# A decoder layer on one NeuronCore: the row of maxima of the cross-attention written by one VectorE step over seven rows of contraction

## What is computed

```python
q = (query @ Wq + bq).reshape(B, Nq, H, D).transpose(0, 2, 1, 3)
k = (key_value @ Wk + bk).reshape(B, Nkv, H, D).transpose(0, 2, 1, 3)
v = (key_value @ Wv + bv).reshape(B, Nkv, H, D).transpose(0, 2, 1, 3)
attn = jnp.einsum('bhqd,bhkd->bhqk', q, k) * scale
attn = jnp.clip(attn, -CLAMP, CLAMP)
attn = jax.nn.softmax(attn, axis=-1)
x = jnp.einsum('bhqk,bhkd->bqhd', attn, v).reshape(B, Nq, Cq)
return x @ Wo + bo
```

## Time and profile before

| | us |
|---|---|
| median of 3 runs | 972.74 |
| lowest, highest | 971.3, 974.29 |
| the profiled execution, its own time | 974.64 |
| its span in the trace | 972.5 |
| TensorE busy | 924.9 (95%) |
| VectorE busy | 699.5 (72%) |
| ScalarE busy | 645.9 (66%) |
| GpSimd busy | 351.0 (36%) |

### The profile page before, as it was taken

How to read it: one execution, slowest core, us unless ns; L and a number is a source line. 1 busy time by engine, 2 the same in 40 slices (tenths; PEclk the granted TensorE clock), 3 DMA queues, 4 the chain that set the end, 5 groups by cost and what they waited for, 6 DMA issues and landing times.

```text
span 972.5 us, 28783 instructions
## 1 busy us (share of the span) xinstructions
PE 924.9 (95%) x10471; PEld 741.4 (76%) x10471; DVE 699.5 (72%) x1490; ACT 645.9 (66%) x1081; POOL 351.0 (36%) x332
## 2 busy tenths in 40 slices
PE   6777999999999999999999999999999999999995
PEld 4655777777777777777777777777777778999894
DVE  6673777767676677676767767767788857777996
ACT  4654777777777777777777777777776545445554
POOL 6452362222333333222233333332222413112992
PEclk8897999999999999999999999999999999999998
DMA  5538566666655555666666555566665201002321
GB/s 141 121 79 191 120 133 140 143 136 137 137 128 119 119 119 126 141 137 138 136 137 134 119 119 119 120 137 143 137 138 111 69 1 44 23 23 86 128 114 41
DMA packets 43626, 111.44 MB, mean 115 GB/s; under 512 B 15491, under 2 KB 26053, under 8 KB 43461
## 3 DMA queue, kind: packets, MB, share of 16 engines
q1 hardware_dynamic: 43572, 110.77, 50.3%
HBM read 32.23 MB, written 1.89 MB: 35 GB/s over the span
## 4 chain that ended last, share of the span: by engine, by line
PE 84%; ACT 5%; DVE 4%; issue 3%; SPq 2%; POOL 1%; DMA 1%; ACTq 0%; DVEq 0%; POOLq 0%
PE psum L1592 17%; PE psum L1424 16%; PE psum L1652 13%; PE psum L1431 8%; PE psum L1436 8%; PE psum L1656 4%; ACT arena L759 3%; PE psum L1679 2%; PE psum L1692 2%; PE psum L1691 2%; PE psum L1680 2%; PE psum L1681 2%; PE psum L1693 2%; PE psum L1441 1%; SPq L396 1%
## 5 line engine op out<-in xcount | busy, mean ns | idle before, releaser
L946 DVE TENSOR_REDUCE arena<-psum 128x1 f32<-128x500 f32 x672 | 447.8, 674 | 210.1 <-PE psum L1424 206.9
L759 ACT ACTIVATE arena<-psum 125x896 f32<-125x896 f32 x384 | 347.5, 916 | 109.0 <-PE psum L1592 101.7
L1424 PE MATMUL psum<-K_hi,Q_bd 128*128 128x500 f32 x672 | 319.6, 485 | 7.0 <-DVE arena L946 4.1
L547 POOL TENSOR_TENSOR arena<-arena,K_hi 128x500 fp32r<-128x500 f32 x96 | 120.7, 1257 | 403.3 <-ACT K_hi L690 403.3
L1592 PEld LDWEIGHTS psum<-Q_st,K_st 97*125 97x125 f32 x1536 | 221.6, 189 | 42.4 <-ACT arena L759 16.6
L1592 PE MATMUL psum<-Q_st,K_st 97*125 97x224 f32 x1536 | 238.6, 278 | 6.1 <-ACT arena L759 5.6
L1652 PE MATMUL psum<-arena 125*25 125x168 f32 x3072 | 170.5, 311 | 0.2
L1424 PEld LDWEIGHTS psum<-K_hi,Q_bd 128*128 128x128 f32 x672 | 128.6, 192 | 53.3 <-issue 20.8
L813 ACT ACTIVATE K_st<-psum 128x448 fp32r<-128x448 f32 x128 | 69.8, 545 | 79.5 <-PE psum L1681 78.0
L1656 PE MATMUL psum<-arena 125*9 125x56 f32 x3072 | 117.6, 213 | 0.0
L1656 PEld LDWEIGHTS psum<-arena 125*9 125x9 f32 x3072 | 94.1, 91 | 16.6
(11 more groups left out here) (249 smaller groups left out, 983.3 us busy)
## 6 DMA issues: line engine op xcount, KB each, us to landing
K_st<-K_hi SPq DMA_DIRECT2D x256, 187.5 KB, 4.8
K_st<-arena SPq DMA_DIRECT2D x128, 187.5 KB, 3.4
arena<-in_ctx SPq DMA_DIRECT2D x32, 562.5 KB, 6.8
arena<-gate_rows SPq DMA_DIRECT2D x8, 896.0 KB, 4.4
arena<-in_L_ffn_W SPq DMA_DIRECT2D x16, 256.0 KB, 3.2
Q_st<-max_row SPq DMA_DIRECT2D x224, 0.5 KB, 1.7
arena<-OS_all SPq DMA_DIRECT2D x12, 168.0 KB, 4.0
x_rows<-x_all SPq DMA_DIRECT2D x1, 896.0 KB, 6.4
```

The source lines that it names most:

```text
L547: g.tensor_tensor(low.bitcast(F32R), low, K_hi[:, par, n * KB:n * KB + KB].bitcast(F32), ALU.subtract).then_inc(F["keys_low"], 1)
L759: a.activation(P2[c % NP].rearrange("p (n k) -> p n k", n=2), psum[0:CK, 2 + 2 * (c % 2):4 + 2 * (c % 2), 0:HQ // 2], ACT.Exp)\
L946: v.reduce_max(mx[:, n // NB, n % NB:n % NB + 1], bank_of(n)[:, 0:KB], AX.X).then_inc(F["piece_max_taken"], 1)
L1424: mm(bank_of(n)[:, 0:KB], Q_bd[:, par].rearrange("p h q -> p (h q)")[:, 128 * (n // NB):128 * (n // NB) + 128], K_hi[:, par, (n % NB) * KB ...
```

## The change

The last row of the contraction becomes seven rows. `K_st` holds 1.0 in rows 96 to 102, and `Q_st` has in row 96 + j the maxima of group j in the 128 columns of that group, negated, and zeros elsewhere, so the sum over the seven rows is the same. These seven rows of 896 columns are written by one VectorE instruction, which reads the turned maxima from bank 1 seven times over and multiplies them by a small mask `minus_blocks` (-1 on the diagonal, 0 off it). The tile `max_row`, the transfers of `load_row` and their semaphore are gone.

For that the turned maxima have to lie in PSUM partitions 96 to 102. `m2x` becomes the last 7 columns of `m2x_wide` (128 x 103, its first 96 columns zero), in fp32r, and `turn` is one matmul in fp32r with 103 columns of weights against an fp32r identity, where it was an fp32 matmul with 7.

The columns of piece maxima `mx` are doubled by parity, so piece 0 of a batch waits for the `row_max` of two batches before. `row_out` waits that the scores of the batch before last, which used the same half of `Q_st`, are made. The places of all steps are given by named constants that have the same values as before (`BEFORE_TURN = 1`, `NEXT = 9`), and the waits of the projections on bank 7 are worked out by a helper `bank_free`, with the same thresholds as before but in the period of batch 30, where it waits for older copies as well.

```diff
-        Q_st = sb("Q_st", [DC + 1, 2, HG, 4, S], F32R)
+        Q_st = sb("Q_st", [DC + RG, 2, HG, 4, S], F32R)
-        max_row = sb("max_row", [RG, 128], F32R)
+        minus_blocks = sb("minus_blocks", [128, RG])
+        ident_r = sb("ident_r", [128, 128], F32R)
+        m2x_wide = sb("m2x_wide", [128, DC + RG], F32R)
-        mx = at(128, RG, NB)
+        mx = at(128, 2, RG, NB)
-        m2x = at(128, RG)
+        m2x = m2x_wide[:, DC:DC + RG]
...
-            sp.wait_ge(F["max_row_ready"], 1 + PRIME)
-            load_row(0)
...
-                if has(b, 1):
-                    sp.wait_ge(F["max_row_ready"], b + 2 + PRIME)
-                    load_row(1 - par)
...
+            step(g.memset(minus_blocks[:], 0.0))
+            keep(minus_blocks[:], [[-1, RG]], -DC, 1, ALU.not_equal, -1.0)
+            step(g.tensor_copy(ident_r[:], ident[:]))
+            step(g.tensor_scalar(m2x_wide[:], ident[:, 0:DC + RG], 0.0, None, ALU.mult))
...
-                if not isinstance(b, int) or b >= 1:
-                    dve.wait_ge(D_["mrow"], b * (16 * RG))
-                v.tensor_scalar(max_row[:], bank[1][0:RG, 0:128], -1.0, None, ALU.mult).then_inc(F["max_row_ready"], 1)
+                if not isinstance(b, int) or b >= 2:
+                    dve.wait_ge(F["scores_made"], (b - 1) * NC + PRIME)
+                v.tensor_tensor(Q_st[DC:DC + RG, par].rearrange("p g h q -> p (g h q)").rearrange("p (j c) -> p j c", c=128),
+                                bank[1][DC:DC + RG, 0:128].unsqueeze(1).to_broadcast([RG, RG, 128]),
+                                minus_blocks[DC:DC + RG].unsqueeze(2).to_broadcast([RG, RG, 128]), ALU.mult).then_inc(F["max_row_ready"], 1)
...
-                mm(bank[1][0:RG, 0:128], m2x, ident[:], start=True, stop=True).then_inc(F["max_transposed"], 1)
+                if more and BEFORE_TURN > 1:
+                    pe.wait_ge(F["piece_max_taken"], (b + 1) * PIECES + BEFORE_TURN - 1 + PRIME)
+                mm(bank[1][0:DC + RG, 0:128], m2x_wide[:], ident_r[:], start=True, stop=True).then_inc(F["max_transposed"], 1)
...
-                            pe.wait_ge(D_["mrow"], (b + 1) * (16 * RG))
+                            pe.wait_ge(F["max_row_ready"], b + 1 + PRIME)
...
-                                      K_st[0:DC + 1, par, g, c * CK:c * CK + CK], Q_st[:, par, g].rearrange("p h q -> p (h q)"), start=True, stop=True)
+                                      K_st[0:DC + RG, par, g, c * CK:c * CK + CK], Q_st[:, par, g].rearrange("p h q -> p (h q)"), start=True, stop=True)
```

More of the change, by code:

```diff
@@ L493, in _ @@
             pool.sem_inc(consts, 1)
[L494 to L495 removed]
+            step(g.memset(K_st[DC:DC + RG, 0, HG - 1].bitcast(F32), 1.0))
+            step(g.memset(K_st[DC:DC + RG, 1].rearrange("p g k -> p (g k)").bitcast(F32), 1.0))
             def later_constants():
@@ L749, in period @@
                 for c in range(NC):
-                    if c == 0 and has(b, -1):
+                    if c == COPY_SLOT and has(b, -1):
                         act.wait_ge(F["outputs_made"], b * NC + PRIME)
@@ L760, in period @@
                          .then_inc(F["weights_ready"], 1)
-                    if c == 9 and has(b, 1):
+                    if c == KEEP_SLOT and has(b, 1):
                         keep_extremes(b + 1)
@@ L975, in _ @@
             for n in range(8):
-                piece_max(0, n)
+                piece_max(0, 0, n)
             first_attended(3)
             for n in range(8, PIECES):
-                piece_max(0, n)
-            row_max(0)
-            row_out(0)
-            for n in range(3):
-                piece_max(1, n)
+                piece_max(0, 0, n)
+            row_max(0, 0)
+            for n in range(BEFORE_TURN - 1):
+                piece_max(1, 1, n)
+            row_out(0, 0)
+            for n in range(max(BEFORE_TURN - 1, 0), BEFORE_TURN + 2):
+                piece_max(1, 1, n)
             dve.wait_ge(w_ps, 2)
@@ L988, in _, with taken @@
             v.memset(bank[6], 0.0).then_inc(F["bank_cleared"], 1)
-            for n in range(3, 9):
-                piece_max(1, n)
-            def taken(b, c, table):
+            for n in range(BEFORE_TURN + 2, NEXT):
+                piece_max(1, 1, n)
+            def taken(b, par, c, table):
                 for ahead, n in pieces(c, table):
@@ L995, in taken @@
                         continue
-                    piece_max(b + ahead, n)
+                    piece_max(b + ahead, (par + ahead) % 2, n)
             def period(b, par, half):
                 for c in range(NC):
-                    taken(b, c, EARLY_PIECES)
-                    taken(b, c, MID_PIECES)
-                    if c == 7 and has(b, 1):
-                        row_max(b + 1)
+                    taken(b, par, c, EARLY_PIECES)
+                    taken(b, par, c, MID_PIECES)
+                    if c == ROW_SLOT and has(b, 1):
+                        row_max(b + 1, 1 - par)
                     if c == TURN_SLOT and has(b, 1):
-                        row_out(b + 1)
+                        row_out(b + 1, 1 - par)
                     if has(b, -1):
-                        if c == SUM_SLOT:
+                        if c == SUM_SLOTS[0]:
                             dve.wait_ge(F["outputs_copied"], b + PRIME)
@@ L1524, in _ @@
             first_query(3)
-            pieces1(0)
-            turn(0)
-            pieces1(1)
+            pieces1(*range(BEFORE_TURN))
+            turn(0, True)
+            pieces1(BEFORE_TURN)
             pe.wait_ge(S1["queries_copied"], NQ)
```

97 lines of the change are left out of this document (51 added, 46 removed).

## The result

The changed kernel takes 965.88 us in the median of 4 runs (965.36 to 966.49), the kernel before, beside it on the same chip, 972.33 us (971.3 to 974.29). The ratio is 0.9931, with a 95% interval from 0.9914 to 0.9949: 6.5 us, or 0.7%, faster. 968.0 had been forecast, with a range from 964 to 972.5. The profiled execution took 966.49 us, 8.15 us less than the profiled one of before.

A forecast was written before the change was run, and what follows sets the result against it. TensorE, busy 95% of the span, was taken as the bound, with SyncE's queue in the chain at the start. Terms -2.2 - 2.6 - 1.0 + 1.0 = -4.8 us took the median 972.74 to 967.9, rounded to 968; range 964 to 972.5.

The forecast's parts named there:

- The queue at the start: SyncE's queue ahead of period 0: without the seven transfers it goes on 2.2 us earlier, bounds 1.8 to 3.1.
- The slide: Start: four added GpSimd constants push back the `K_st` memset and everything after by 1.1 us (0.6 to 1.3), 0.9 kept.
- TensorE's stop: Start, wait for batch 1's keys: shortens from 6.16 to 2.2 us, less half-clock loss; gain 2.6 us, bounds 0 to 4.6.
- The turn: Turn of the maxima on TensorE: one matmul instead of two gains 0.03 us in each of 31, 1.0 us.
- what streaming gives back, the load takes: Turn: loading 103 weight columns instead of 7, not fetched ahead, nearly cancels what the single matmul saves.
- The rival that had three quarters of the turn come off: Turn: the 103-column load hides behind the piece in front, 0.14 us a turn, 4.3 us in all: 964.6 us; chance 0.08.
- `row_out`, 0 in the middle and 1.0 us at the end: VectorE's `row_out` grows to 1.06 us: hidden in 28 middle periods, costs 1.0 us (0.5 to 1.5) in batches 28 to 30.
- The knee: Middle periods: from 1.14 us on, `row_out` makes TensorE wait in slot 9; each further 0.1 us costs 0.1 us.
- The rest: 103 contraction rows, doubled `mx`, `row_out`'s new wait and the slack of SyncE's later transfers: no time gained or lost.
- the clock doesn't fall: Start, behind TensorE's shortened stop: the clock stays up and gives 4.6 us, time 965.9 us; chance 0.2.
- only the stop gets shorter: Start: the clock falls and stays low as long as before, gain 2.2 us, time 970.5 us; chance 0.15.
- The long `row_out`: Middle periods: `row_out` takes 1.75 us, 0.6 too long, 17 us in all, time 985 us; chance 0.12.

The follow-up runs named there:

- the edit alone: The changed kernel with its four GpSimd constants behind the `K_st` memset instead of ahead of it: 966.33 us, ratio 0.9919.
- the three edits together: The changed kernel with the constants behind the memset, piece 0 of batch 1 reduced ahead of `row_out`, and low keys' transfers ahead of the queries': 961.88 us, ratio 0.9873.
- the two: The changed kernel with piece 0 of batch 1 reduced ahead of `row_out` and the low keys' transfers ahead of the queries': 964.62 us, ratio 0.9885.
- the early keys alone: Batch 1's low keys' transfers ahead of the queries' on SyncE's queue: changed kernel 966.16 us, ratio 0.9915; kernel before, also ahead of the row's seven, 973.92 us, 1.0001.
- two more edits: Added to reduction first and early low keys on the changed kernel: constants behind the memset, VectorE's copies and bank 6 clearing behind its reductions: 959.74 us, ratio 0.9861.

## Why the prediction came out right

The time lay in the range, 2.1 us below the forecast. The loop's and the queue's parts were right in kind; at the start a part of the reasoning was wrong, and that the sum came out near is partly luck. Against the profiled execution the sum was -4.8 us where the traces show -8.2: 0.9 us too little for the start, 2.0 to 2.4 too little for the turn, 0.3 too much for the end, and 0.2 behind it.

*The queue at the start, 2.2 us.* Right in kind, and with the seven transfers put back the time rose by 6 us. The keys landed 84.83 - 82.69 = 2.14 us earlier, as forecast, but in part by luck: the queries' transfers started only 1.58 us earlier and those out of `K_lo` 1.04, and the rest is that these landed sooner behind their issue, for which no cause is shown. The slide was mis-sized: the memset moved by 1.42 us (12.38 to 13.80), beyond my bound of 1.3, because each of the four constants costs its own 0.1 to 0.5 us and a gap behind it. That it carries through to the end of VectorE's step held: in all fourteen profiles the step ends 0.03 us behind the memset (18.93 and 18.98 in the two of the changed kernel, for 17.50), also in two in which it starts 0.05 us ahead of the memset, and takes 5.2 us. So it doesn't matter there which of the two starts first. That part of the slide comes back (0.9 us kept of 1.1) was a guess, and wrong: where the low clock lies alike, all of it reaches the first turn, 61.84 for 60.39.

*TensorE's stop, 2.6 us.* Size in its bounds, mechanism missed. From the landing to the turn of batch 1 it is 4.78 us instead of 7.20, and to `row_out` of batch 2 27.56 instead of 31.17: 3.6 us, 0.1 of it the turn's. But there was no stop of 2.2 us at 81. I added `row_out`'s 0.8 us to the first pieces as a shift of work. In fact it stands between the turn and the reduction of piece 0 of batch 1, and made a stop of 1.99 us on TensorE there, at 62.06 to 64.05; behind this one the clock fell, from 65.6 to 75.8 instead of from 81.1 to 94.7. It fell there, for 10.2 us, in each of the seven profiles with a stop of 1.99 us or more at this place. I had weighed two stops (1.85 us without a fall, 2.36 with one) to price the stop that I expected, and did not look for a new one in the stretch where the longer step stands first in line.

*The turn, 0.03 us.* Too small by a factor of about four: 0.11 us by the period, 0.13 by the chain, 3.0 to 3.4 us instead of 1.0. The step that failed is "what streaming gives back, the load takes". The load does start behind `row_max`, as said, and takes 0.17 us, but 7 or 103 columns make no difference to the period: it is 22.06 us in the kernel with the turn alone edited, and 22.06 in the changed one. The rival that had three quarters of the turn come off (0.14 us) was nearly right on the turn, but not by its reason, a load that hides behind the piece in front: this one starts behind `row_max`, as before. Why its extra 0.08 us doesn't show stays open. This surplus of 2.0 to 2.4 us is the largest part of what the sum missed.

*`row_out`, 0 in the middle and 1.0 us at the end.* Right: 1.10 us for 1.06, no wait in the middle (0.5 us in two late periods in all), 0.73 us at the end. The knee, priced at 1.14 us, lies at about 1.10 by the run with the longer `row_out`: 0.62 us more gave 0.60 us a period. At some 1.21 us a call, 0.11 behind the knee, the loop's gain would have been gone, by the same estimate.

*The rest, nothing.* Held, in that the profile has the loads of the scores at 189 ns with 103 rows as with 97.

*The rivals.* That the clock doesn't fall gave 965.9, the time that was measured, but the clock did fall, elsewhere, so the match is chance. That only the stop gets shorter (970.5) did not come about either, since the stop went. The long `row_out` is shown to cost about what it was priced at, 985 us at 1.75 us a call (985.7 measured, with two steps of 1.70 us together), had it been that long. The Trainium skill (SBUF — State Buffer, Who interferes with whom) says that a VectorE step with at most one input in SBUF, outside the modes that use two ports, doesn't contend with GpSimd. This trace agrees: the 32 calls, one input in PSUM, took 1.096 to 1.098 us.

Partly open: why the kernel before, and versions with row transfers on the queue at the start, scatter over 5 to 10 us (969 to 980) and the changed one over 2. The granted clock on record for each execution says where the time goes. Of the 29 executions of the kernel before on the first chip, the six longest (977.6 to 979.5 us) have a mean of 0.979 or 0.980, the six shortest (969.4 to 972.3) 0.982 to 0.989. A difference of 0.01 is 19 us more at 1.2 GHz, up to 10 us of work lost. What makes the clock fall in one execution and not in the next isn't shown; that TensorE waits for a landing at the start fits it, but the long ones have no trace. Open too is whether the memset's 1.4 us are worth anything in the median: the edit alone says no, the three edits together beat the two by 0.0012 in the ratio, less than either's interval.

## What to carry to other kernels

Where a start-up stretch has several limits in a row, one edit can show nothing, and its result then says little about the edit: the early keys alone were worth nothing measurable, on both kernels. With the row off the queue and the reduction put first they brought the second turn 2.5 us closer to the first, and with two more edits the median fell by 6.5 us. Look for what is late next before you judge, and test edits together.

A small transfer isn't cheap for being small. Seven of 0.5 KB held an in-order queue for 4.8 us, and in a busy stretch (DMA share above 1.0) took 6.9 us to land, where the median over the program is 1.7; a VectorE step of 1.1 us in the shadow of other work replaced them. And where a step gets longer, look at each place where it runs, not only at the loop's: ask who stands behind it in the prologue.

## What the runs showed of the hardware

- After a stop of 1.99 us (ending at 64.05) TensorE's clock went from 2.4 to 1.2 GHz and came back 10.2 us later, TensorE being busy nearly all the time. So it was in all six profiles with this stop, and in the one in which it is 2.60 us.
- After a wait of 1.03 us some 5 us behind the first turn, in the six profiles that have one, the clock fell for 3.4 us in three profiles, for 6.8 us in one, and stayed at 1.00 in two, both of the kernel before or a version of it.
- After a stop of 2.26 us (ending at 84.97) it stayed as well. A stop that ends at 19.1 was followed by 6.8 or 3.4 us at half clock in two executions of one kernel. The length of a stop alone does not tell whether the clock falls, or for how long.
- The move from two fp32 matmuls of 0.27 us to one fp32r matmul of 0.22 us in the turn took 0.11 us off the period, while the load of 103 columns instead of 7, 0.08 us longer, took nothing back.
- VectorE's `tensor_scalar` on 112 x 4 elements, which overlaps GpSimd's memset of 5.09 us, ends 0.03 us behind it in all fourteen profiles, and takes from 3.5 to 5.2 us, depending on when it starts.
- A memset of 7 partitions takes as long as one of a single partition: 5.09 us for 6000 columns in both kernels.
